# Who issues the stores of the weights' low parts: ScalarE, or the sync engine

## The chip, the cores and the metric

The kernel runs on one core of a Trainium2 chip. The metric is the time of one execution on the device in microseconds (us), median of several runs. The engines are TensorE (PE in the rows, PEld for its weight loads), VectorE (DVE), ScalarE (ACT), GpSimd (POOL) and the sync engine (SP), which here only issues DMAs. A "q" behind an engine's name (SPq, ACTq) marks what its sequencer does, such as issuing a DMA.

## What is computed

A cross-attention layer with a residual, then a mixture of experts with a residual. There are 2 x 1024 tokens of width 256, a context of 77 tokens per batch, 16 heads, 8 experts of which each token takes 2, and an inner width of 512:

```python
qp = jnp.einsum('bld,ed->ble', q, Wq)
scores = jnp.einsum('bld,bmd->blm', qp, kv)
idx = jnp.argmax(scores, axis=-1)
mem = jnp.take_along_axis(kv, idx[..., None], axis=1)
mkv = jnp.einsum('bld,ed->ble', mem, Wkv)
...
h = jnp.einsum('td,eid->tei', x, w1)
gate = jax.nn.silu(h[..., :INTER])
y = h[..., INTER:] * gate
out = jnp.einsum('tei,ehi,te->th', y, w2, combine)
...
x = x + _L0_xattn_ref(_layernorm(x, axis=-1), ctx_1024, L0_xattn_Wq, L0_xattn_Wkv, L0_xattn_Wc)
x = x + _L0_ffn_ref(_layernorm(x, axis=-1), L0_ffn_w1, L0_ffn_w2, L0_ffn_router_w)
```

`combine` holds the two largest router probabilities of each token. The expert products are made from split operands: a weight is a rounded high part in `W` (fp32r) and a remainder in bf16, the low part.

## The kernel before

**Two phases.** The first is attention and router, over `NH` = 4 groups of 512 tokens. The second takes 39 blocks of 128 gathered rows, each with one expert. It needs all weights in both parts.

**Slots.** In the first phase PE, DVE and ACT each run through a hand-written order: `for u in range(-1, NH + 1): for p in range(SLOTS)` with `SLOTS` = 10. In turn u the engines work on the logits and sums of group u, prepare group u + 1 and finish group u - 1 (`post`). Slot s here means (u + 1) * 10 + p. Each engine works in its own order and waits on semaphores; no engine looks ahead past a wait.

**The weights' split.** The expert weights come in as `NC` = 48 chunks of 128x512 fp32 (`raw`). In slot n, as the last thing of the slot, ACT's `high(n)` copies chunk n, rounded, to `W` (line 481) and raises `hi_ok`. GpSimd's split n (line 411) subtracts it from `raw` and writes the low part to buffer n % 2 of `low`, raising `low_ok`. `W` lies two chunks before `raw` in the same memory, so copy n overwrites what split n - 2 reads: copy n has to come behind split n - 2. Two slots later `high(n + 2)` issues the store of low part n to `lows` in DRAM (line 477, 128 KB) from ACT's queue. GpSimd's split n + 2 writes the same buffer and waits until that store has landed (`low_out`). GpSimd also makes a reciprocal root (line 428) once per group, between the splits of slots 23 and 24, 33 and 34, 43 and 44: it feeds the normalisation on DVE (line 719).

**The sync engine** first issues all input loads (the 48 raw chunks as 8 transfers), then two stores of padding (lines 341 and 342). Then for v = 0, 1, 2 it runs `keep_residual(v)` and `keep_rows(v)`: it waits for group v's residual sum (`x2_ok`, made in slot 10v + 24) and stores 512 KB from `X`, then waits for its router result (`rows_ok`, made by DVE's line 761 in slot 10v + 30) and stores 528 KB from `xr`. Behind them it waits for all low stores and loads the low parts of the first weights back to `W1lo` (line 362); it stores the last group's residual, loads the low parts of the second weights (line 369) and stores the last rows. The second phase starts when PE has all of this and GpSimd's first gathers (line 448) have landed.

Of the kernel before, what the change touches and what calls it, by code (L numbers as in the profile page):

```python
# [24 lines left out]
F32 = mybir.dt.float32  # L25
F32R = mybir.dt.float32r
F16 = mybir.dt.float16
BF16 = mybir.dt.bfloat16
I32 = mybir.dt.int32
U32 = mybir.dt.uint32  # L30
ALU = mybir.AluOpType
ACT = mybir.ActivationFunctionType
AX = mybir.AxisListType
ds = bass.ds

P = 128
# [7 lines left out]
NH = T // HT  # L44
# [11 lines left out]
BLK = 2 * S * B // P + E - 1  # L56
GR = 4
LAST = (BLK - 1) // GR
CW = 512
WC1 = DC * 2 * FI // CW  # L60
WC2 = FC * D // CW
EC = WC1 + WC2
NC = E * EC
SCALE = 0.25
MASK = -1e30
EPS = 1e-5
assert HT >= GR and DH ** -0.5 == SCALE


SLOTS = NP + 2  # L70
# [7 lines left out]
P2_AT = 4  # L78
# [14 lines left out]
def build(nc, x, ctxT, Wq, WqT, WkvT, WcT, routerT, w, out):  # L93
    rows = nc.dram_tensor("rows", [(T + 1) * P, RW], F32).ap()
    lows = nc.dram_tensor("lows", [NC, P, CW], BF16).ap()
    with ExitStack() as ctx:
        def sb(name, shape, dt=F32):
            return ctx.enter_context(nc.sbuf_tensor(name, shape, dt))

        def sem(name):  # L100
            return ctx.enter_context(nc.semaphore(name))
# [77 lines left out]
        idf = sb("idf", [P, BLK])  # L179
        idx = sb("idx", [P, BLK], U32)  # L180

        low = sb("low", [P, 2, CW], BF16)


        with nc.sbuf_tensor("raw", [P, NC + 2, CW], F32) as raw:
# [1 line left out]
        W = sb("W", [P, NC + 2, CW], F32R)  # L187
# [45 lines left out]
        raw_in = [sem(f"raw_in{e}") for e in range(E)]  # L233
        hi_ok = sem("hi_ok")
        low_ok = sem("low_ok")
        low_out = [sem(f"low_out{i}") for i in range(2)]
        low_in = sem("low_in")
        iotas = sem("iotas")
        consts = sem("consts")
# [86 lines left out]
        @block.sync  # L326
        def _(sp):
            sp.dma_start(X[:, 0:TB, :], x[0:S, :].rearrange("(t p) d -> p t d", p=P)).then_inc(x_in[0], 16)
            sp.dma_start(CT, ctxT.rearrange("(c p) n -> p c n", p=P)).then_inc(wts_in, 16)
            sp.dma_start(WQ[:], Wq.rearrange("(c p) n -> p c n", p=P)).then_inc(wts_in, 16)  # L330
            sp.dma_start(WKV[:], WkvT.rearrange("(c p) n -> p c n", p=P)).then_inc(wts_in, 16)
            sp.dma_start(WQT[:], WqT.rearrange("(c p) n -> p c n", p=P)).then_inc(wts_in, 16)
            sp.dma_start(WC[:], WcT.rearrange("(c p) n -> p c n", p=P)).then_inc(wts_in, 16)
            sp.dma_start(RT[:], routerT.rearrange("(c p) n -> p c n", p=P)).then_inc(wts_in, 16)
            sp.dma_start(X[:, TB:T, :], x[S:2 * S, :].rearrange("(t p) d -> p t d", p=P)).then_inc(x_in[1], 16)
            for e in range(E):
                sp.dma_start(raw[:, 2 + e * EC:2 + (e + 1) * EC, :], w[e * EC:(e + 1) * EC].rearrange("n p w -> p n w")
                             ).then_inc(raw_in[e], 16)

            sp.wait_ge(pad_ok, 1)  # L340
            sp.dma_start(rows[T * P:(T + 1) * P, :], xr[:, 0, :]).then_inc(rows_out, 16)
            sp.dma_start(out[T * P:(T + 1) * P, :], xr[:, 0, 0:D]).then_inc(rows_out, 16)

            def keep_residual(v):
                sp.wait_ge(x2_ok, v * 2 + 2)
                sp.dma_start(out[ds(v * (HT * P), HT * P), :].rearrange("(t p) d -> p t d", p=P),
                             X[:, ds(v * HT, HT), :]).then_inc(x2_out, 16)

            def keep_rows(v):
                sp.wait_ge(rows_ok, v + 1)  # L350
                sp.dma_start(rows[ds(v * (HT * P), HT * P), :].rearrange("(t p) d -> p t d", p=P),
                             xr[:]).then_inc(rows_out, 16)

            with sp.Fori(0, NH - 1) as v:
                keep_residual(v)
                keep_rows(v)

            for j in range(2):
                sp.wait_ge(low_out[j], 16 * NC // 2)
            sp.wait_ge(l2_mm, NH * NP)  # L360
            for e in range(E):
                sp.dma_start(W1lo[:, e * WC1:(e + 1) * WC1, :],
                             lows[e * EC:e * EC + WC1].rearrange("n p w -> p n w")).then_inc(low_in, 16)
            keep_residual(NH - 1)

            sp.wait_ge(x2_out, 16 * NH)
            sp.wait_ge(xn2_ok, T)
            for e in range(E):
                sp.dma_start(W2lo[:, e * WC2:(e + 1) * WC2, :],
                             lows[e * EC + WC1:(e + 1) * EC].rearrange("n p w -> p n w")).then_inc(low_in, 16)  # L370
            keep_rows(NH - 1)


        @block.gpsimd
        def _(pool):
            def iota(t, pattern, mult=0, start=0):
                pool.iota(t, pattern=pattern, base=start, channel_multiplier=mult,
                          allow_small_or_imprecise_dtypes=True).then_inc(iotas, 1)

            iota(iota_f[:], [[1, P]])  # L380
            iota(iota_p[:], [[0, 1]], 1)
            iota(iota_h[:], [[1, P]])
            iota(blk_h[:], [[1, BLK]])
            iota(blk_f[:], [[1, BLK]])
            iota(tok_h[:], [[P, T]], 1, 1)
            iota(k128[:], [[P, T]])
            iota(desc[:], [[-1, NK]], 0, NK)
            iota(desc_e[:], [[-1, E]], 0, E)
            iota(cum[:], [[1, E], [-1, E]])
            iota(spare[:], [[0, 1]], 1, T * P + 1)  # L390
            pool.memset(half[:], -0.5).then_inc(iotas, 1)

            pool.wait_ge(iotas, 12)
            for b in range(B):
                pool.wait_ge(ln_v, b + 1)
                pool.tensor_tensor(rs[:, b * TB:(b + 1) * TB], rs[:, b * TB:(b + 1) * TB], half[:, 0:TB], ALU.pow
                                   ).then_inc(ln_r, 1)

            def split(i, j, first):
                n = i * 2 + j
                pool.wait_ge(iotas, 12)
                pool.wait_ge(hi_ok, n + 1)
                if not first:
                    pool.wait_ge(low_out[j], i * 16)
                if first:
                    was, high = raw[:, n + 2, :], W[:, n, :]
                else:
                    was, high = (a.rearrange("p a w -> p (a w)") for a in (raw[:, ds(n + 2, 1), :], W[:, ds(n, 1), :]))  # L410
                pool.tensor_tensor(low[:, j, :], was, high.bitcast(F32), ALU.subtract).then_inc(low_ok, 1)  # L411

            def splits(start, stop):
                with pool.Fori(start // 2, stop // 2) as i:
                    for j in range(2):
                        split(i, j, False)

            for j in range(2):
                split(0, j, True)
            done = 2  # L420
            for v in range(NH):

                until = min(NC, (v + 2) * SLOTS + P2_AT)
                if until > done:
                    splits(done, until)
                    done = until
                pool.wait_ge(v2_ok, v + 1)
                pool.tensor_tensor(rs2[:], rs2[:], half[:, 0:HT], ALU.pow).then_inc(rs2_ok, 1)

            pool.wait_ge(idx_ok, 1)
            pool.wait_ge(rows_out, 16 * (2 * B + 2))
            pool.wait_ge(x2_out, 16 * 2 * B)

            def at_rows(b):
                return bass.IndirectOffsetOnAxis(ap=idx[:, b:b + 1], axis=0)

            for b in range(BLK + GR):
                if b >= GR:  # L440
                    c = b - GR
                    pool.wait_ge(ob_ok, c + 1)
                    if c >= 1:
                        pool.wait_ge(sc_out, 16 * c)
                    pool.indirect_dma_start(out=out, out_offset=at_rows(c), in_=ob[:, c % GR, :], in_offset=None,  # L445
                                            compute_op=ALU.add).then_inc(sc_out, 16)
                if b < BLK:
                    pool.indirect_dma_start(out=xg[:, b % GR, :], out_offset=None, in_=rows, in_offset=at_rows(b)  # L448
                                            ).then_inc(g_in[b % GR], 16)
            pool.wait_ge(sc_out, 16 * BLK)  # L450
# [3 lines left out]
        def _(act):  # L454
# [16 lines left out]

            def high(n):

                if 2 <= n < NC + 2:

                    act.wait_ge(low_ok, n - 1)
                    act.dma_start(lows[n - 2], low[:, n % 2, :]).then_inc(low_out[n % 2], 16)
                if n < NC:
                    if n % EC == 0:
                        act.wait_ge(raw_in[n // EC], 16)  # L480
                    act.copy(W[:, n, :], raw[:, n + 2, :]).then_inc(hi_ok, 1)  # L481
# [92 lines left out]
            step(0, True, False)  # L574
            with act.Fori(1, LAST) as i:
                step(i, False, False)
# [666 lines left out]
```

## Time and profile before

| what | value |
|---|---|
| median of 3 runs | 467.67 us (467.65 to 468.54) |
| span of the profiled execution | 468.0 us |
| PE busy | 376.7 us, 80% |
| DVE busy | 221.9 us, 47% |
| ACT busy | 197.3 us, 42% |
| GpSimd busy | 171.6 us, 37% |

The profile is one execution, recorded instruction by instruction. Its chain of waits is followed back from the last instruction: at each step to what released it. Times in the timelines are us from the start of the span. The first phase ends at about 234 us, the second begins at about 251 us. A row of a timeline gives start, duration, engine, line, operation, output and inputs, how many, and in brackets how long the engine sat idle before and what released it. PEclk is the granted clock of TensorE as a share of full speed; about 0.5 is 1.2 GHz and 1.0 is 2.4 GHz.

### The profile page before, as it was taken

How to read it: one execution, taken by the hardware profiler on the slowest of the kernel's cores; microseconds unless marked ns; L12 is line 12 of the kernel's file. 1: busy time of each engine (PE TensorE's matmuls, PEld its weight loads, DVE VectorE, ACT ScalarE, POOL GpSimd, SP SyncE). 2: the span in 40 equal slices, each digit the busy share in tenths (PEclk: the TensorE clock that was granted, in tenths of full speed). 3: DMA queues.
4: the chain of work that ended last, by engine and by line, in shares of the span. 5: the costliest groups of instructions: out<-in, count | busy, mean ns of one | idle time of the engine just before them, and what ended most of it. 6: DMA issues, size and time to landing. Idle time of an engine off the chain costs nothing.

```text
span 468.0 us, 7576 instructions
## 1 busy us (share of the span) xinstructions
PE 376.7 (80%) x2262; PEld 282.8 (60%) x2263; DVE 221.9 (47%) x535; ACT 197.3 (42%) x376; POOL 171.6 (37%) x148
## 2 busy tenths in 40 slices
PE   1758688879999988765514999999999999999980
PEld 1647565558677655343513677777777777677760
DVE  4576734545674764543382344344344344343430
ACT  0324546666657664420101444444444444344330
POOL 2021633433333353320003245545545545544521
PEclk9967979999979998876555999999999999999986
DMA  8999110111212112229611032332332332332320
GB/s 266 386 387 336 57 34 34 46 45 35 69 45 82 68 57 87 73 91 349 223 48 46 8 62 47 57 57 46 55 59 46 51 63 46 47 67 46 50 32 11
DMA packets 35317, 43.44 MB, mean 93 GB/s; under 512 B 3200, under 2 KB 27904, under 8 KB 35296
## 3 DMA queue, kind: packets, MB, share of 16 engines
q1 hardware_dynamic: 20896, 26.49, 16.5%
q0 software_dynamic: 7488, 10.39, 13.6%
q10 hardware_dynamic: 6912, 6.29, 4.0%
q8 instruction: 12, 0.20, 0.2%
q14 instruction: 9, 0.07, 0.0%
HBM read 27.23 MB, written 15.93 MB: 92 GB/s over the span
## 4 chain that ended last, share of the span: by engine, by line
PE 74%; DVE 12%; ACT 4%; issue 4%; DMA 2%; POOL 1%; SPq 1%; DVEq 0%; POOLq 0%; ACTq 0%
PE ps L1155 24%; PE ps L1166 12%; PE ps L1173 4%; PE ps L985 4%; PE ps L972 4%; PE ps L1064 3%; PE ps L998 3%; PE ps L1017 3%; PE ps L1019 3%; PE ps L1032 3%; PE ps L1045 2%; PE ps L1141 2%; PE ps L1078 2%; ACT qs L509 1%; PE ps L943 1%
## 5 line engine op out<-in xcount | busy, mean ns | idle before, releaser
L445 POOL DMA_INDIRECT out_x<-oT,idx x39 | 61.8, 1586 | 98.8 <-ACT oT L558 98.8
L411 POOL TENSOR_TENSOR low<-raw,W 128x512 bf16 (+1 forms) x48 | 62.0, 1295 | 95.4 <-DMA lows<-low 79.6
L1155 PE MATMUL ps<-W,qs 128*128 x312 | 83.6, 411 | 1.2 <-DVE qs L884 1.2
L1155 PEld LDWEIGHTS ps<-W,qs 128*128 128x128 f32 x312 | 57.4, 191 | 13.2 <-issue 1.6
L890 DVE TENSOR_TENSOR uT<-uT,ps 128x512 f32<-128x512 f32 x39 | 26.8, 687 | 69.9 <-ACT uT L564 69.9
L564 ACT ACTIVATE uT<-ps 128x512 f32<-128x512 f32 x39 | 23.4, 599 | 85.9 <-PE ps L1155 85.9
L448 POOL DMA_INDIRECT xr<-rows,idx x39 | 38.7, 991 | 38.5 <-DVE idx L874 26.9
L894 DVE TENSOR_TENSOR qs<-ps,mT 128x512 fp32r<-128x512 f32 x39 | 27.0, 692 | 49.3 <-ACT mT L570 49.3
L1155 PE MATMUL ps<-W1lo,xpT 128*128 x156 | 41.3, 388 | 0.0
L693 DVE TENSOR_REDUCE mx<-ps 128x8 f32<-128x616 f32 x32 | 25.5, 798 | 32.7 <-PE ps L998 32.6
L488 ACT ACTIVATE pT<-ps 77x1024 f32<-77x1024 f32 x32 | 32.7, 1022 | 13.7 <-PE ps L1019 13.7
L985 PE MATMUL ps<-ident,qs 128*128 128x128 f32 x128 | 21.9, 297 | 13.5 <-DVE qs L684 8.8
L1166 PE MATMUL ps<-W,mT 128*128 x156 | 28.7, 307 | 2.0 <-DVE xpT L895 2.0
L481 ACT CAST W<-raw 128x512 fp32r<-128x512 f32 x48 | 29.8, 621 | 0.2
L1017 PE MATMUL ps<-qT,bd 128*77 128x512 f32 x64 | 29.3, 458 | 0.5 <-ACT pT L488 0.3
L558 ACT ACTIVATE oT<-ps,xr 128x256 f32<-128x256 f32 x39 | 18.5, 474 | 24.2 <-PE ps L1166 23.3
L1173 PE MATMUL ps<-ident,uT 128*128 128x128 f32 x156 | 24.3, 278 | 5.0 <-issue 3.9
L985 PEld LDWEIGHTS ps<-ident,qs 128*128 128x128 f32 x128 | 15.5, 151 | 19.6 <-DVE qs L684 16.8
L1019 PE MATMUL ps<-mT,neg 128*77 128x512 f32 x64 | 26.1, 408 | 0.0
L1166 PE MATMUL ps<-W,qs 128*128 x156 | 25.3, 285 | 0.0
L998 PEld LDWEIGHTS ps<-bd,qT 128*128 128x128 f32 x128 | 19.9, 203 | 8.6 <-issue 4.2
L494 ACT CAST qT<-ps 128x512 fp32r<-128x512 f32 x32 | 18.8, 587 | 14.4 <-PE ps L985 14.3
(171 smaller groups left out, 641.9 us busy)
## 6 DMA issues: line engine op xcount, KB each, us to landing
raw<-in_w SPq DMA_DIRECT2D x8, 1536.0 KB, 17.0
lows<-low ACTq DMA_DIRECT2D x48, 128.0 KB, 1.7
W1lo<-lows SPq DMA_DIRECT2D x8, 512.0 KB, 7.7
rows<-xr SPq DMA_DIRECT2D x4, 528.0 KB, 3.3
X<-in_x SPq DMA_DIRECT2D x2, 1024.0 KB, 6.9
out_x<-X SPq DMA_DIRECT2D x4, 512.0 KB, 3.3
X<-lows SPq DMA_DIRECT2D x8, 256.0 KB, 4.4
xr<-rows,idx POOLq DMA_INDIRECT x39, 2.8
```

The lines of the kernel that those rows point to most:

```text
L411: pool.tensor_tensor(low[:, j, :], was, high.bitcast(F32), ALU.subtract).then_inc(low_ok, 1)
L445: pool.indirect_dma_start(out=out, out_offset=at_rows(c), in_=ob[:, c % GR, :], in_offset=None, compute_op=ALU.add).then_inc(sc_out, 16)
L448: pool.indirect_dma_start(out=xg[:, b % GR, :], out_offset=None, in_=rows, in_offset=at_rows(b)).then_inc(g_in[b % GR], 16)
L481: act.copy(W[:, n, :], raw[:, n + 2, :]).then_inc(hi_ok, 1)
L488: act.activation(pT[0:NK, 2 * (n % 4):2 * (n % 4) + 2, :], ps[0:NK, 0:2, :], ACT.Exp).then_inc(ex_ok, 1)
L985: mm = pe.transpose(ps[:, 5, n * P:(n + 1) * P], qs[:, a:a + 2, :].rearrange("p h w -> p (h w)"), ident[:])
L998: mm = pe.matmul(ps[:, 6 + n // 2, (n % 2) * 2 * NK:(n % 2 + 1) * 2 * NK], qT[:, w % 2, 4 * g + n, t * P:(t + 1) * P], bd[:, w // 2, :], s ...
L1017: pe.matmul(ps[0:NK, o, :], bd[:, u // 2, o * NK:(o + 1) * NK], qT[:, u % 2, p, :], start=True, stop=False)
L1019: mm = pe.matmul(ps[0:NK, o, :], neg[:, 2 * p + o:2 * p + o + 1].broadcast_to([P, NK]), mT[:], start=False, stop=True)
L1155: mm = pe.matmul(ps[:, f, :], part[:, c * P:(c + 1) * P], chunk(wts, e * per + (2 * c + f)), start=(k == 0 and c == 0), stop=(k == 2 and c ...
L1166: mm = pe.matmul(ps[:, 4, 0:D], part[:, c * P:(c + 1) * P], w2, start=(k == 0 and c == 0), stop=(k == 2 and c == FC - 1))
L1173: mm = pe.transpose(ps[:, 3, c * P:(c + 1) * P], yb[:, c * P:(c + 1) * P], ident[:])
```

## The change

ACT's `high(n)` no longer issues stores. It keeps the wait on `low_ok` in front of copy n, because of the overlap of `W` and `raw`. The sync engine issues the 48 stores instead, each behind a wait on `low_ok`, written out between its other transfers: 22 stores before the first residual, then 4, the first rows, 6, the second residual, 4, the second rows, 6, the third residual, 4, the third rows, and the last 2. The number of buffers has a name now, `LR`, and stays 2. GpSimd's splits are written out one by one instead of in a loop; each waits for `hi_ok` and for the store of the part two before.

```diff
+            def keep_lows(start, stop):
+                for n in range(start, stop):
+                    sp.wait_ge(low_ok, n + 1)
+                    sp.dma_start(lows[n], low[:, n % LR, :]).then_inc(low_out[n % LR], 16)
+
+            kept = 0
+            for v in range(NH - 1):
+                keep_lows(kept, min(NC, (v + 2) * SLOTS + 2))
                 keep_residual(v)
+                keep_lows(min(NC, (v + 2) * SLOTS + 2), min(NC, (v + 2) * SLOTS + P2_AT + 2))
+                kept = min(NC, (v + 2) * SLOTS + P2_AT + 2)
                 keep_rows(v)
-
-            for j in range(2):
-                sp.wait_ge(low_out[j], 16 * NC // 2)
+            keep_lows(kept, NC)
+
+            for j in range(LR):
+                sp.wait_ge(low_out[j], 16 * NC // LR)
...
             def splits(start, stop):
-                with pool.Fori(start // 2, stop // 2) as i:
-                    for j in range(2):
-                        split(i, j, False)
-
-            for j in range(2):
-                split(0, j, True)
-            done = 2
+                for n in range(start, stop):
+                    pool.wait_ge(hi_ok, n + 1)
+                    if n >= LR:
+                        pool.wait_ge(low_out[n % LR], 16 * (n // LR))
+                    pool.tensor_tensor(low[:, n % LR, :], raw[:, n + 2, :], W[:, n, :].bitcast(F32), ALU.subtract
+                                       ).then_inc(low_ok, 1)
+
+            done = 0
...
             def high(n):

-                if 2 <= n < NC + 2:
-
-                    act.wait_ge(low_ok, n - 1)
-                    act.dma_start(lows[n - 2], low[:, n % 2, :]).then_inc(low_out[n % 2], 16)
                 if n < NC:
+                    if n >= 2:
+                        act.wait_ge(low_ok, n - 1)
                     if n % EC == 0:
                         act.wait_ge(raw_in[n // EC], 16)
                     act.copy(W[:, n, :], raw[:, n + 2, :]).then_inc(hi_ok, 1)
```

The sync engine's instructions from the padding to the loads of `W1lo`, before (lines 346 to 351 are a loop of three turns):

```order
L341 DMA rows<-xr 128x264 [waits pad_ok]
L342 DMA out_x<-xr 128x256
L354 UNCONDITIONAL_BRANCH
L354 ISA
L346 ISA [waits x2_ok]
L346 REGISTER_ALU
L346 DMA out_x<-X 128x4x256
L350 REGISTER_ALU
L351 ISA [waits rows_ok]
L351 DMA rows<-xr 128x4x264
```

The same stretch of the changed kernel, up to the second rows (its lines are two or more further down):

```order
L343 DMA rows<-xr 128x264 [waits pad_ok]
L344 DMA out_x<-xr 128x256
L359 DMA lows<-low 128x512 [waits low_ok] x22
L348 DMA out_x<-X 128x4x256 [waits x2_ok]
L359 DMA lows<-low 128x512 [waits low_ok] x4
L353 DMA rows<-xr 128x4x264 [waits rows_ok]
L359 DMA lows<-low 128x512 [waits low_ok] x6
L348 DMA out_x<-X 128x4x256 [waits x2_ok]
L359 DMA lows<-low 128x512 [waits low_ok] x4
L353 DMA rows<-xr 128x4x264 [waits rows_ok]
```

Low parts 26 and 27 now stand behind the first rows (`rows_ok`), 36 and 37 behind the second, 22 and 23 behind the first residual, and the first low part stands behind the two stores of padding.

ACT at the end of slot 30 and in slot 31, before (`qT` and `qs` belong to the preparation of group 3, `pT` to the exponentials of group 2):

```order
L477 DMA lows<-low 128x512 [waits low_ok]
L481 CAST W<-raw 128x512 [waits raw_in5]
L494 CAST qT<-ps 128x4x128 [waits q_tr]
L488 ACTIVATE pT<-ps 77x1024 [waits pv_mm,l2_mm]
L509 CAST qs<-ps 128x16x2x16 [waits q_tr,q_mm]
L516 COPY oT<-ps 128x512 [waits o_tr]
L477 DMA lows<-low 128x512 [waits low_ok]
L481 CAST W<-raw 128x512
```

And in the changed kernel:

```order
L480 CAST W<-raw 128x512 [waits raw_in5,low_ok]
L493 CAST qT<-ps 128x4x128 [waits q_tr]
L487 ACTIVATE pT<-ps 77x1024 [waits pv_mm,l2_mm]
L508 CAST qs<-ps 128x16x2x16 [waits q_tr,q_mm]
L515 COPY oT<-ps 128x512 [waits o_tr]
L480 CAST W<-raw 128x512 [waits low_ok]
```

The issues are gone, and the wait on `low_ok`, which stood on the issue, now stands on the copy; what follows the copy is unchanged.

## Rows read from the trace of the kernel before

**Rows 1.** The page: the chain of waits by engine, and GpSimd's splits.

```profile
PE 74%; DVE 12%; ACT 4%; issue 4%; DMA 2%; POOL 1%; SPq 1%; DVEq 0%; POOLq 0%; ACTq 0%
...
L411 POOL TENSOR_TENSOR low<-raw,W 128x512 bf16 (+1 forms) x48 | 62.0, 1295 | 95.4 <-DMA lows<-low 79.6
```

**Rows 2.** The page's DMA issues: count, KB each, median us to landing.

```profile
lows<-low ACTq DMA_DIRECT2D x48, 128.0 KB, 1.7
...
rows<-xr SPq DMA_DIRECT2D x4, 528.0 KB, 3.3
...
out_x<-xr SPq DMA_DIRECT2D x1, 128.0 KB, 11.9
```

**Rows 3.** Timeline, slots 30 and 31, group 0's router result.

```profile
139.02 0.62 ACT L481 CAST W<-raw 128x512 fp32r<-128x512 f32 x1
...
139.54 0.58 ACT L494 CAST qT<-ps 128x512 fp32r<-128x512 f32 x1
...
139.72 0.19 DVE L761 TENSOR_TENSOR xr<-ex,sme 128x32 f32<-128x32 f32 x1
...
140.08 0.39 SPq L351 DMA_DIRECT2D rows<-xr  x1
...
140.55 1.02 ACT L488 ACTIVATE pT<-ps 77x1024 f32<-77x1024 f32 x1 [0.43 <-PE ps L1019]
...
141.86 0.58 ACT L509 CAST qs<-ps 128x512 fp32r<-128x512 f32 x1 [0.29 <-PE ps L972]
...
142.96 0.66 PE L985 MATMUL ps<-ident,qs 128*128 128x128 f32 x4 [0.70 <-DVE qs L684]
```

**Rows 4.** Timeline, the start: the stores of padding, splits 2 and 3.

```profile
34.76 2.75 SPq L342 DMA_DIRECT2D out_x<-xr  x1
...
47.27 2.55 POOL L411 TENSOR_TENSOR low<-raw,W 128x512 bf16 x2 [4.14 <-DMA lows<-low]
```

**Rows 5.** Windows: busy per engine, PEclk, DMA share, GB/s, behind 194 us.

```profile
194.00:198.00 4.00, 3.39 (x16) 1.86 (x16) 1.15 (x4) 1.63 (x3) 0.00 (x0) 0.57 0.12 37
```

**Rows 6.** Timeline, slots 40 and 41, group 1's router result.

```profile
170.62 1.31 DVE L740 TENSOR_TENSOR eq<-rl,r 128x32 f32<-128x32 f32 x1
...
172.28 0.62 ACT L481 CAST W<-raw 128x512 fp32r<-128x512 f32 x1
...
174.57 1.02 ACT L488 ACTIVATE pT<-ps 77x1024 f32<-77x1024 f32 x1 [1.67 <-PE ps L1019]
...
177.75 0.19 DVE L761 TENSOR_TENSOR xr<-ex,sme 128x32 f32<-128x32 f32 x1
...
177.91 0.78 PE L1017 MATMUL ps<-qT,bd 128*77 128x512 f32 x1
```

**Rows 7.** Timeline: splits 39 and 40 beside the router, and the router step alone.

```profile
133.16 0.18 DVE L740 TENSOR_TENSOR eq<-rl,r 128x32 f32<-128x32 f32 x1
...
172.78 2.51 POOL L411 TENSOR_TENSOR low<-raw,W 128x512 bf16 x2 [0.90 <-DMA lows<-low]
```

**Rows 8.** Timeline: residual stores, splits and normalisation of groups 0 and 2.

```profile
117.74 0.42 SPq L346 DMA_DIRECT2D out_x<-X  x1
...
121.54 1.37 DVE L719 TENSOR_SCALAR xr<-X,mv,rs 128x256 f32<-128x256 f32 x4
...
189.24 0.38 SPq L346 DMA_DIRECT2D out_x<-X  x1
...
191.23 2.53 POOL L411 TENSOR_TENSOR low<-raw,W 128x512 bf16 x2
...
191.29 3.26 DVE L719 TENSOR_SCALAR xr<-X,mv,rs 128x256 f32<-128x256 f32 x4 [0.38 <-POOL rs L428]
```

**Rows 9.** Timeline, the end of the first phase and the first gather.

```profile
207.96 7.83 SPq L362 DMA_DIRECT2D W1lo<-lows  x8
...
224.51 3.97 SPq L369 DMA_DIRECT2D X<-lows  x8
...
248.23 1.19 POOL L448 DMA_INDIRECT xr<-rows,idx  x1 [26.92 <-DVE idx L874]
```

More of the change, by code:

```diff
@@ L58 @@
 LAST = (BLK - 1) // GR
+LR = 2
 CW = 512
@@ L66 @@
 EPS = 1e-5
+assert NC % LR == 0
 assert HT >= GR and DH ** -0.5 == SCALE
@@ L180, in build @@
         idx = sb("idx", [P, BLK], U32)
-        low = sb("low", [P, 2, CW], BF16)
+        low = sb("low", [P, LR, CW], BF16)
         with nc.sbuf_tensor("raw", [P, NC + 2, CW], F32) as raw:
@@ L235, in build @@
         low_ok = sem("low_ok")
-        low_out = [sem(f"low_out{i}") for i in range(2)]
+        low_out = [sem(f"low_out{i}") for i in range(LR)]
         low_in = sem("low_in")
@@ L352, in keep_rows @@
                              xr[:]).then_inc(rows_out, 16)
-            with sp.Fori(0, NH - 1) as v:
+            def keep_lows(start, stop):
[5 more added lines that the diff above has]
+                keep_lows(kept, min(NC, (v + 2) * SLOTS + 2))
                 keep_residual(v)
+                keep_lows(min(NC, (v + 2) * SLOTS + 2), min(NC, (v + 2) * SLOTS + P2_AT + 2))
+                kept = min(NC, (v + 2) * SLOTS + P2_AT + 2)
                 keep_rows(v)
-            for j in range(2):
-                sp.wait_ge(low_out[j], 16 * NC // 2)
+            keep_lows(kept, NC)
+            for j in range(LR):
+                sp.wait_ge(low_out[j], 16 * NC // LR)
             sp.wait_ge(l2_mm, NH * NP)
@@ L397, in _ @@
                                    ).then_inc(ln_r, 1)
[L401 to L411, printed above, removed]
-            def splits(start, stop):
-                with pool.Fori(start // 2, stop // 2) as i:
-                    for j in range(2):
-                        split(i, j, False)
-            for j in range(2):
-                split(0, j, True)
-            done = 2
+            def splits(start, stop):
+                for n in range(start, stop):
[5 more added lines that the diff above has]
+            done = 0
             for v in range(NH):
```

## The prediction, made before the changed kernel ran

> **What bounds the kernel now.** I read the chain of waits by engine first: TensorE holds 74% of it, VectorE 12%, ScalarE 4%, and all DMAs 2% [rows 1]. So the stores of the low parts aren't what ends the time, although the splits sat idle for 79.6 us behind them: GpSimd is not on the path, and most of that idle time is free. The second thing to see is the order of one slot. ScalarE's copy of chunk n is followed by work that TensorE waits for within a microsecond or two [rows 3]. If the copy is late, TensorE is late. Before the change a store waited only for its own low part and for ScalarE's turn, never for the sync engine's other work.
>
> **What the change takes away.** 48 issues on ScalarE. In the trace an issue lies beside the activation ahead of it, and the copy starts about half a microsecond behind that activation's start with or without it. I put 0.0 to 0.1 us on each, and nearly all of ScalarE's slots have idle time in front of their next step, so of a possible 4.8 us I count 0.3 us as gained. GpSimd's splits start about a microsecond earlier, since a store leaves when the part is ready; that by itself shortens nothing, as they are off the chain.
>
> **What it moves: low parts 26, 27, 36 and 37 behind the rows.** This is the large term. The sync engine issues in order. It reaches the store of part 26 only after it has issued the first rows, and those wait for DVE's line 761 in slot 30. Split 28 writes the buffer of part 26, so it waits for that store. Copy 30 overwrites what split 28 reads, so it waits for split 28. ScalarE's copy 30 stands ahead of its `qT`, exponential and `qs` steps of slot 31. Step by step for group 0 [rows 3]:
> Line 761 ends at 139.91 us. The splits 28 and 29, which ran beside that router chain before, now wait; where a split ran beside it, steps of it were 1 us long instead of 0.2 [rows 7]. Here a late matmul ahead of it bounds it, so I move it by only 0.15 us, and the rows are issued at 139.9. They land 3.3 us later [rows 2]. Part 26 follows on the same queue, 0.4 us of further transfer (its 128 KB at the pace of the 512 KB): 143.6. The split takes 1.27 us, with 0.15 us for each of two semaphores: copy 30 starts at 145.2 instead of 139.02, and `qT` at 145.7. Now the exponential, which waited for TensorE before, follows at once: 146.2, and `qs` at 147.2 instead of 141.86. TensorE's next transposes (142.96) need it, so they come **5.3 us later**. The other side: if the store of part 26 doesn't queue behind the rows, it lands 0.4 + 1.7 us after them, at 142.0, and the delay is 3.7 us. I take 5.3, because a transfer of 128 KB that stood behind others on this queue, the padding's, took 11.9 us to land where one on ScalarE's queue took 1.7 [rows 2].
> The Trainium skill ("DMA: Bandwidth & Descriptors", section "Queues, rings and completion order") says that a DMA engine takes descriptors in ring order within a queue and goes round-robin between the queues of different issuers; the same section warns that completion is not first-in-first-out. By the first the delay is 5.3 us, by the second alone it could be the 3.7 us; the 11.9 us row agrees with the first.
>
> **TensorE's clock after the stop.** TensorE stands for some 6 us there. Behind a shorter stop (TensorE waited there for the normalisation that ended at 194.55) the granted clock was 0.57 for 4 us [rows 5, 8], about the lower level of 1.2 GHz. 4 us at 0.57 instead of 1.0 cost 4 x 0.43 = **1.7 us**. The bounds are 0 (it was already low shortly before, in slots 28 and 29) and twice that.
>
> **Group 1, slot 40.** The same four steps with other numbers [rows 6]. Copy 40 was made at 172.28, but line 761 only at 177.75, 5.5 us later: the chain of the router ran beside splits 37 to 40, and three of its steps take 1.1 to 1.3 us there, as the one of 1.31 us [rows 6], which takes 0.18 alone [rows 7]. In the changed kernel splits 38 to 40 can't run there, so this chain is about 3.0 us shorter: rows issued at 175.0 (in times of the old trace), part 36 landed at 178.7, split 38 done at 180.1, copy 40 at 180.2. The exponential, before at 174.57, comes at 180.7 and ends at 181.7; TensorE's next logits need it and start at 181.75 instead of 177.91: **3.8 us later**. So here the gain on DVE is already netted. Without that gain it would be 6.8, without queueing behind the rows 2.2. The low clock comes once in either case.
> On this collision the Trainium skill ("SBUF — State Buffer", section "Who interferes with whom") says that DVE's `tensor_tensor` with two SBUF inputs and GpSimd's reads lock each other out for a whole instruction; the rows agree, 1.2 us being about one split.
>
> **Low parts behind the residuals.** Parts 22, 32 and 42 wait for the residual's issue and then for its 512 KB: 3.3 + 0.4 = 3.7 us. For group 2 this is a gain. The residual goes at 189.24, so split 44 starts at about 193.0. Before, splits 44 and 45 ran at 191.23, beside the normalisation at 191.29, which took 3.26 us instead of the 1.37 of group 0 [rows 8]. It becomes free: 1.9 us, and TensorE's stop behind it shrinks by as much, so that the low clock behind it should not come: its 3.39 busy us at 0.57 [rows 5] would be 1.5 us shorter. Copy 46 then waits half a microsecond for split 44. Together **-2.9 us** (0 to -3.4). For groups 0 and 1 it is the other way round: the residual at 117.74 plus 3.7 is 121.4, and the normalisation stands at 121.54. Splits 24 and 25 now fall on it. It would take up to 3.26 instead of 1.37 us, of which TensorE's order hides about 0.9: **+1.0 us each, +2.0** (0 to 2.5).
>
> **The start.** Part 0 is now issued behind the padding. That was issued at 34.76 and landed 11.9 us later, at 46.7 [rows 2, 4]. Part 0 lands at about 47.1, and split 2, which before started at 47.27, starts at about the same time [rows 4]. I count 0; if the queue is 2 us longer than that, copy 4 stops and it costs up to 2 us. The splits of slots 4 to 7 move against a DVE chain there: -0.5 to +0.5, counted as 0.
>
> **The end.** Parts 46 and 47 go behind the last rows, so the loads of `W1lo` start 4 us later than 207.96. The first gather is at 248.23 [rows 9], and the last of all loads is issued by 228.5; this cover of some 20 us, less a landing of about 5, hides them, and I count 0. Were it gone, the 4 us would be paid in full.
>
> **The sum**: 5.3 + 1.7 + 3.8 - 2.9 + 2.0 - 0.3 = 9.6 us on the profiled span of 468.0 us, so 477.6. The median is 0.33 lower than that span, and I take 0.3 off for it: 477.3 us.
>
> **Rivals.**
> *The store doesn't queue behind the rows.* The pause is real, but the two stops are 3.7 and 2.2 instead of 5.3 and 3.8: 474.1. Splits 24 and 34 then run earlier and miss the normalisation: 472. Against it stands the padding's 11.9 us.
> *The start backs up as well.* The padding's issue alone took 2.75 us [rows 4], so the queue is full there. Two to three us more: 480.
> *The change does what it says*, each store goes when its part is there, and nothing waits for rows. It can't for parts 26, 27, 36 and 37: the order of the sync engine's instructions is fixed. It could only be harmless if ScalarE had enough idle time, but 0.43 and 0.29 us stand in slot 31 [rows 3]. That gives no change, 467.7.
> *Faster: DVE freed of the splits decides.* One mechanism: the splits are held back just where they lay beside the router and the normalisation. At slot 40 this gives 3.0 us and at 191 us 2.9, so 462 us if the stops cost nothing. It decides if the split that ends a stop comes less than about 1 us after the router's result, against the 5.1 us worked out.
>
> **How the numbers follow.** The forecast of 477.3 has 0.70, the rival without queueing 0.14 (472 to 474), the backed-up start 0.07, no effect 0.03, faster 0.06. The range takes in the forecast with its bounds (the clock term 0 to 3.4, the collisions 0 to 2.5) and the upper part of the rival without queueing: 472 to 481. A measurement of this kernel can tell about 0.2%, or 0.9 us, from no change. Slower by more than that: 0.91; same 0.04; faster 0.05.
>
> **What would show it.** In the changed kernel's timeline: copies 30 and 40 each directly behind a split, that split directly behind a low store, that one behind the rows, with TensorE idle for about 6 us at slot 31 and 7 us at slot 41. The router steps of 1.2 us at slot 40 should be gone and the normalisation of group 2 back at 1.4 us, those of groups 0 and 1 longer. The landing of parts 26 and 36 should be some 3.3 us after their issue, others 1.7. I'd be wrong if those copies are not late, if part 26 lands in 1.7 us, or if TensorE finds other work.

## The result, and the profile after

The changed kernel took 478.0 us in the median of 4 runs (474.94 to 481.15), beside 468.11 us (467.65 to 472.69) of the kernel before: a ratio of 1.0152, 95% interval 1.0099 to 1.0204. Ratios and their intervals here are taken from executions in the chip's faster state alone and are not the quotient of the two medians, which would be 1.021. The profiled execution has a span of 477.6 us, 9.6 us more than the 468.0 of before.

The page of the changed kernel: the chain of waits by engine, GpSimd's splits and ScalarE's copies (now lines 418 and 480), and two kinds of DMA issues.

```profile
PE 73%; DVE 12%; ACT 4%; DMA 3%; issue 3%; POOL 1%; SPq 1%; DVEq 0%; ACTq 0%; POOLq 0%
...
L418 POOL TENSOR_TENSOR low<-raw,W 128x512 bf16<-128x512 f32 x48 | 61.4, 1285 | 104.5 <-ACT W L480 71.8
...
L480 ACT CAST W<-raw 128x512 fp32r<-128x512 f32 x48 | 29.8, 620 | 13.3 <-POOL low L418 13.1
...
lows<-low SPq DMA_DIRECT2D x48, 128.0 KB, 1.7
...
rows<-xr SPq DMA_DIRECT2D x4, 528.0 KB, 3.0
```

Against [rows 1] most splits no longer wait for a store but for ScalarE's copy (71.8 us): the stores do leave when their part is there. GpSimd is off the path in both kernels. The third row is the price: ScalarE sat idle 13.1 us in front of its copies because of a split, 2 times. Before, its copies had no such wait.

The first of the two, slot 30, in the timeline of the changed kernel (it answers to [rows 3]):

```profile
142.50 0.19 DVE L760 TENSOR_TENSOR xr<-ex,sme 128x32 f32<-128x32 f32 x1
...
142.72 0.37 SPq L353 DMA_DIRECT2D rows<-xr  x1
...
146.20 2.48 POOL L418 TENSOR_TENSOR low<-raw,W 128x512 bf16<-128x512 f32 x2 [12.98 <-DMA lows<-low]
...
147.49 0.62 ACT L480 CAST W<-raw 128x512 fp32r<-128x512 f32 x1 [5.58 <-POOL low L418]
...
149.41 0.58 ACT L508 CAST qs<-ps 128x512 fp32r<-128x512 f32 x1
...
150.50 1.11 PE L984 MATMUL ps<-ident,qs 128*128 128x128 f32 x4 [5.39 <-DVE qs L683]
```

Read the brackets from the top: split 28 waited 12.98 us for a store, copy 30 waited 5.58 us for the split, TensorE waited 5.39 us for the step behind the copy, where it had waited 0.70. Part 26 was issued at 143.13 and landed 2.9 us later. The second, slot 40 (it answers to [rows 6]):

```profile
185.37 0.19 DVE L760 TENSOR_TENSOR xr<-ex,sme 128x32 f32<-128x32 f32 x1
...
189.07 2.48 POOL L418 TENSOR_TENSOR low<-raw,W 128x512 bf16<-128x512 f32 x2 [9.44 <-DMA lows<-low]
...
190.37 0.62 ACT L480 CAST W<-raw 128x512 fp32r<-128x512 f32 x1 [7.56 <-POOL low L418]
...
191.96 0.71 PE L1016 MATMUL ps<-qT,bd 128*77 128x512 f32 x1 [6.54 <-ACT pT L487]
```

TensorE's clock behind the two stops, in the windows of the changed kernel (busy us and count of PE, PEld, DVE, ACT, POOL, then PEclk, DMA share, GB/s; compare [rows 5]):

```profile
145.50:150.50 5.00, 0.00 (x0) 0.00 (x1) 0.48 (x2) 3.01 (x6) 3.66 (x3) 0.87 0.25 82
150.50:154.50 4.00, 4.00 (x15) 3.36 (x16) 0.64 (x2) 2.10 (x3) 1.37 (x2) 0.50 0.21 68
154.50:158.50 4.00, 4.00 (x26) 2.77 (x24) 1.23 (x2) 2.99 (x5) 1.28 (x1) 0.81 0.01 2
...
191.90:195.90 4.00, 3.69 (x10) 2.29 (x11) 0.00 (x0) 2.91 (x6) 2.51 (x2) 0.50 0.27 93
```

TensorE did nothing for 5 us; then it worked for 4 us without a gap at 0.50, its lower level of 1.2 GHz, and had 0.81 over the next 4 us. In the kernel before, the clock was 1.00 over the same steps (142.96 to 154 us). Together that is 4 x 0.50 + 4 x 0.19 = 2.8 us of work, about the 2.6 us of the table below.

The shift of ScalarE's copies (copy n is the one of slot n) against the trace of before shows where the 9.6 us of this execution came from:

| stretch | shift at its end | what it added |
|---|---|---|
| start to slot 29 | +2.8 | 0.45 for group 0's normalisation, -0.4 at slot 18, and 2.8 that did not come again in the second trace (see `after_again`) |
| first stop, to the `qs` step of slot 31 | +7.5 | +4.7 |
| to copy 33 | +10.1 | +2.6, low clock |
| to copy 39 | +10.3 | +0.2, of it 0.45 for group 1's normalisation |
| second stop, to the logits of slot 41 | +14.0 | +3.7, with a router chain 2.7 us shorter |
| to copy 43 | +14.8 | +0.8, low clock |
| to the first gather | +11.7 | -3.1, group 2's normalisation |
| to the end | +9.6 | -2.1, not explained |

### The profile page after: what moved, and what is told of

It reads as the page before. It is cut to its first block, busy times and chain, and to the rows that moved or that the text cites. A ratio compares the mean times of both kernels' runs of the same rounds, so it can differ in the third digit from the quotient of the medians.

```text
span 477.6 us, 7363 instructions
## 1 busy us (share of the span) xinstructions
PE 379.3 (79%) x2262; PEld 286.0 (60%) x2263; DVE 218.5 (46%) x535; ACT 196.8 (41%) x376; POOL 171.3 (36%) x148
## 4 chain that ended last, share of the span: by engine, by line
PE 73%; DVE 12%; ACT 4%; DMA 3%; issue 3%; POOL 1%; SPq 1%; DVEq 0%; ACTq 0%; POOLq 0%
PE ps L1154 23%; PE ps L1165 11%; PE ps L1172 4%; PE ps L984 4%; PE ps L1063 4%; PE ps L971 4%; PE ps L1031 3%; PE ps L1016 3%; PE ps L997 3%; PE ps L1018 3%; PE ps L1044 2%; PE ps L1140 2%; PE ps L1077 2%; DVE xr L718 2%; PE ps L942 2%
## 5 line engine op out<-in xcount | busy, mean ns | idle before, releaser
L418 POOL TENSOR_TENSOR low<-raw,W 128x512 bf16<-128x512 f32 x48 | 61.4, 1285 | 104.5 <-ACT W L480 71.8
L1154 PE MATMUL ps<-W,qs 128*128 x312 | 83.2, 410 | 1.2 <-DVE qs L883 1.2
L984 PE MATMUL ps<-ident,qs 128*128 128x128 f32 x128 | 24.1, 320 | 17.9 <-DVE qs L683 13.5
L480 ACT CAST W<-raw 128x512 fp32r<-128x512 f32 x48 | 29.8, 620 | 13.3 <-POOL low L418 13.1
L984 PEld LDWEIGHTS ps<-ident,qs 128*128 128x128 f32 x128 | 17.1, 163 | 24.2 <-DVE qs L683 21.5
L997 PE MATMUL ps<-bd,qT 128*128 128x154 f32 x128 | 21.2, 292 | 5.2 <-DVE mx L692 4.1
```

The source lines that it names most:

```text
L418: pool.tensor_tensor(low[:, n % LR, :], raw[:, n + 2, :], W[:, n, :].bitcast(F32), ALU.subtract).then_inc(low_ok, 1)
L984: mm = pe.transpose(ps[:, 5, n * P:(n + 1) * P], qs[:, a:a + 2, :].rearrange("p h w -> p (h w)"), ident[:])
L997: mm = pe.matmul(ps[:, 6 + n // 2, (n % 2) * 2 * NK:(n % 2 + 1) * 2 * NK], qT[:, w % 2, 4 * g + n, t * P:(t + 1) * P], bd[:, w // 2, :], s ...
L1154: mm = pe.matmul(ps[:, f, :], part[:, c * P:(c + 1) * P], chunk(wts, e * per + (2 * c + f)), start=(k == 0 and c == 0), stop=(k == 2 and c ...
```

## The experiments

**The changed kernel again**, beside the three that follow. No edit.

> The changed kernel once more, on the chip of the three below. Order theory (a low part that stands behind the rows stops ScalarE's copies 30 and 40): copies 30 and 40 again directly behind a split, TensorE idle some 5.4 us at slot 31 and 6.5 us at slot 41; 475 to 480 us. The +2.8 us that the changed kernel already had before slot 30 and the -2.1 us of its second phase would be scatter of TensorE's clock: they should come out with other sizes here. If they belong to the change they come again.

Measured: 480.28 us (476.58 to 482.17) beside 470.52 of before, ratio 1.0183 (1.0085 to 1.0282). Line 760 of slot 30 ended 0.1 us later than in the trace of before, not 2.8. So most of those 2.8 us are scatter of one execution: 0.7 us were there at copy 0 already, and of the rest 1.2 us came between copies 9 and 11, with a clock of 0.51 from 57 to 71 us where the kernel before had 0.76. The two traces of before differ in the same way: from copy 0 to the first gather they took 214.6 and 217.4 us. From copy 29 on all came again: copies 30, 31, 33 and 40 at +5.8, +4.9, +7.5 and +15.5. The -2.1 us of the second phase came again too (217.5 us beside 219.8). The span of this execution is 474.8 us, 6.8 us above that of before and 1.4 us above that of the second trace of before (473.4): the total of a single execution is a poor measure here, and the stretches between copies are a good one.

**The low parts ahead of the rows.** The sync engine's order:

```diff
-                keep_lows(min(NC, (v + 2) * SLOTS + 2), min(NC, (v + 2) * SLOTS + P2_AT + 2))
-                kept = min(NC, (v + 2) * SLOTS + P2_AT + 2)
+                keep_lows(min(NC, (v + 2) * SLOTS + 2), min(NC, (v + 3) * SLOTS))
+                kept = min(NC, (v + 3) * SLOTS)
                 keep_rows(v)
```

> As the changed kernel, but the sync engine stores the low parts up to 29 (39) before it waits for the first (second) rows; the residuals keep their place. Order theory: copies 30 and 40 come right behind the step ahead of them, no stop of TensorE over 2.7 us; group 2's normalisation still free (1.4 us), groups 0 and 1's 2.8 and 1.8 us; 466 us (before 467.9, minus 2.9 for group 2, plus 0.9 for the two others). Issuer theory (the loss comes from the sync engine's queue, or from splits that now start earlier, whatever the order): 476 us or more. No-gain case of the forecast's DVE term: 469.

Measured: 464.91 us (463.09 to 465.98), ratio to before 0.9832 (0.9737 to 0.9926). Expected was 2 us less than before; in the medians of this job it is 5.6 us less, more than my terms give. Its timeline at slot 30:

```profile
141.71 0.62 ACT L480 CAST W<-raw 128x512 fp32r<-128x512 f32 x1
...
142.41 1.29 POOL L418 TENSOR_TENSOR low<-raw,W 128x512 bf16<-128x512 f32 x1 [2.65 <-ACT W L480]
...
142.44 1.30 DVE L760 TENSOR_TENSOR xr<-ex,sme 128x32 f32<-128x32 f32 x1
...
143.77 0.37 SPq L353 DMA_DIRECT2D rows<-xr  x1
```

The copy waits for nobody. The same sync engine issues the same 48 stores through the same queue; putting the low parts ahead of the rows is worth 13 us of the first phase in the traces (223.6 and 210.6 us from copy 0 to the first gather) and 15 in the medians. The issuer theory falls. One sees the collision as well: the last step of the router chain lies beside a split and takes 1.30 us instead of 0.19.

**Wait for the rows, but store the low parts first.**

```diff
+                sp.wait_ge(rows_ok, v + 1)
+                keep_lows(min(NC, (v + 2) * SLOTS + P2_AT + 2), kept)
                 keep_rows(v)
```

(with `kept` two higher).

> As the changed kernel, but behind the wait for the rows' result the two waiting low parts go first and the 528 KB of the rows after them. So the wait stays and only the queueing behind the transfer goes. If both make the stop (3.2 us from the rows' issue to the landing of part 26, of which a low store alone takes 1.7): part 26 lands 1.7 us after its issue, each stop is 1.5 us shorter, 474.5 us. If the wait alone makes it: as the changed kernel, 477.5. If the queueing alone makes it: 467 to 469.

Measured: 474.71 us (472.5 to 481.68), ratio 1.0067 (1.0013 to 1.0122), and the changed kernel in the same job 1.0183.

```profile
141.61 0.79 SPq L359 DMA_DIRECT2D lows<-low  x2
142.45 0.45 SPq L353 DMA_DIRECT2D rows<-xr  x1
143.47 2.48 POOL L420 TENSOR_TENSOR low<-raw,W 128x512 bf16<-128x512 f32 x2 [9.71 <-DMA lows<-low]
...
144.76 0.62 ACT L482 CAST W<-raw 128x512 fp32r<-128x512 f32 x1 [4.16 <-POOL low L420]
...
147.77 1.11 PE L986 MATMUL ps<-ident,qs 128*128 128x128 f32 x4 [4.17 <-DVE qs L685]
```

From the sync engine's first issue to the split it is 1.86 us here, and 3.48 us in the changed kernel. Of the difference of 1.6 us, 0.4 us is that the rows' issue no longer comes first, and 1.2 us that part 26 lands 1.7 us after its issue instead of 2.9: the queueing behind the rows' 528 KB. TensorE's stop is 4.17 instead of 5.39 us. So the stop has both causes, and the wait is the larger one.

**No store of a low part waits for anything but its own split:** the low parts also go ahead of the residual.

```diff
-                keep_lows(kept, min(NC, (v + 2) * SLOTS + 2))
+                keep_lows(kept, min(NC, (v + 2) * SLOTS + P2_AT))
                 keep_residual(v)
```

(with the rows as in `rows_last`).

> As rows_last, and the low parts up to 23 (33, 43) go before the residual too, so that no low part waits for anything but itself. Order theory with the collisions: splits 24, 25, 34, 35 run before the normalisation of groups 0 and 1 (1.4 us again), but 44 and 45 fall on group 2's again (3.3 us instead of 1.4, and the low clock behind it); about 468 us, the same as the kernel before. If the collisions cost nothing it is equal to rows_last within 0.5 us. Issuer theory: 476 us or more.

Measured: 465.78 us (462.88 to 466.42), ratio 0.9843 (0.9746 to 0.9939), 2 us less than I expected and the same as `rows_last` within their scatter. Groups 0 and 1's normalisation took 2.35 us, not the 1.4 expected: splits 24 and 34 come ahead of it now, but 25 and 35 follow at once. The collision that I expected at group 2 is there:

```profile
189.76 2.53 POOL L418 TENSOR_TENSOR low<-raw,W 128x512 bf16<-128x512 f32 x2
189.83 3.26 DVE L718 TENSOR_SCALAR xr<-X,mv,rs 128x256 f32<-128x256 f32 x4 [0.39 <-POOL rs L429]
...
193.15 0.66 PE L1044 MATMUL ps<-ident,xr 128*128 128x128 f32 x4 [2.76 <-DVE xr L718]
```

and its first phase is 2.6 us longer than that of `rows_last` (213.2 and 210.6 us from copy 0 to the first gather). Between single executions that scatter by 2.8 us this alone would prove little. But from copy 45 to the first gather, where group 2's normalisation lies, `both_last` takes as long as before (+0.02 us) and `rows_last` 3.1 us less, and the next one shows the same.

**GpSimd held for the normalisation**, on `both_last`:

```diff
                 pool.tensor_tensor(rs2[:], rs2[:], half[:, 0:HT], ALU.pow).then_inc(rs2_ok, 1)
+                if done < NC:
+                    pool.wait_ge(xn2_ok, (v + 1) * HT)
```

> As both_last, and GpSimd waits for the group's normalisation (xn2_ok) before it goes on with splits 24, 34 and 44. Collision theory: the normalisation takes 1.4 us in all groups, so group 2's 3.3 us of both_last and the low clock behind it go (3 us), and groups 0 and 1's 2.35 us too (0.3 us each): 462 us where both_last has 465.8. The other side: the held splits come 2 us later and stop copy 26, 36 or 46; then 466 or more.

> The kernel free once more beside before, in five rounds: 463 to 465 us and a ratio of 0.98 to 0.99 to before. If its distance was that chip's scatter, the ratio is within 0.995 to 1.005.

Measured: 463.88 us (462.86 to 465.05), ratio 0.983 (0.977 to 0.9891), and again 462.75 us (460.49 to 464.94), ratio 0.9845 (0.9794 to 0.9895), six runs on another chip. From the second trace:

```profile
191.08 1.38 DVE L720 TENSOR_SCALAR xr<-X,mv,rs 128x256 f32<-128x256 f32 x4 [0.39 <-POOL rs L429]
192.51 0.66 PE L1046 MATMUL ps<-ident,xr 128*128 128x128 f32 x4 [0.87 <-DVE xr L720]
192.53 2.53 POOL L418 TENSOR_TENSOR low<-raw,W 128x512 bf16<-128x512 f32 x2 [1.49 <-DVE xr L720]
```

TensorE's wait goes from 2.76 to 0.87 us, and from copy 45 to the first gather this trace takes 3.2 us less than before, where `both_last` took as long. This version has the lowest medians; it beats the kernel before by 1.6% and the changed one by about 3%. That it beats `rows_last` or `both_last` in the time is not shown: the intervals overlap.

**GpSimd's splits written out alone**, the stores still issued by ScalarE: the kernel before with the changed kernel's `splits`.

> The kernel before with GpSimd's splits written out one by one, as in the changed kernel, and nothing else: ScalarE issues the stores. Order theory: this part of the change does nothing, 468 to 470 us on a chip on which before has 468 to 470, within 0.3% of it; the splits still start behind the stores. If the written-out splits are what makes rows_last and both_last 1.6% faster than before, this has it too, 463 us.

Measured: 470.08 us, ratio 0.9999 (0.9956 to 1.0042). Within 0.4% this part of the change does nothing to the time. So the 1.6% of `both_last` are not due to the written-out splits; by exclusion they come with the move of the issues to the sync engine. What in that move brings them is open (see the last section).

**The kernel before again.**

> The kernel before once more, for a second trace of it. In the changed kernel and its three variants the stretch from the first gather to the end took 217.1 to 217.8 us, in the one trace of before 219.8. If that is scatter of the clock, a second trace of before shows some 217.5 us; if it belongs to ScalarE's issues it shows 219.8 again. Time by the timing: equal to before, within 0.5%.

Measured: 473.93 us (469.96 to 477.25), ratio 1.0022 (0.9975 to 1.0069). The second phase took 219.5 us, near the 219.8 of the first trace. That does not make it a matter of ScalarE's issues, as my expectation had it: in `only_first` and `only_second` below, where the sync engine issues all stores, it took 219.2 and 219.5 us. More under "what the runs showed".

**A third buffer.**

```diff
-LR = 2
+LR = 3
```

(three small arrays of the routing are laid into `pT` to make room; nothing is computed otherwise).

> The changed kernel with LR = 3, in its own order of the sync engine's stores (three small routing arrays are laid into pT to make room). Order theory: split 28 has a buffer of its own, split 29 waits for the store of part 26, so copy 31 waits where copy 30 did; it was due 2.7 us behind the rows' issue and is ready 5 us behind it. Each stop shrinks from 4.7 and 6.5 us to 2 to 3 us, some 4.5 us less in all: 473 us. If the stop is not due to the buffer behind the rows: as the changed kernel, 477.5 or more.

Measured: 478.21 us (477.03 to 478.86), ratio 1.0145 (1.0086 to 1.0203) on a chip on which before had 471.48. The time missed my 473.

```profile
143.78 0.37 SPq L351 DMA_DIRECT2D rows<-xr  x1
...
147.24 3.86 POOL L416 TENSOR_TENSOR low<-raw,W 128x512 bf16<-128x512 f32 x3 [10.79 <-DMA lows<-low]
148.66 0.62 ACT L478 CAST W<-raw 128x512 fp32r<-128x512 f32 x1 [1.46 <-POOL low L416]
...
190.11 3.78 PE L1061 MATMUL ps<-WC,oT 128*128 128x256 f32 x8
...
200.80 3.26 DVE L716 TENSOR_SCALAR xr<-X,mv,rs 128x256 f32<-128x256 f32 x4 [0.37 <-POOL rs L427]
```

The stop moved by one slot, as expected: copy 31 waits now, 1.46 us instead of the 5.58 of copy 30. Over both stops (copies 29 to 33 and 39 to 43) the trace lost 2.3 us against before, where the changed kernel lost 11.7. But the spare buffer also takes the protection from group 2: split 44 no longer waits behind the residual and falls on the normalisation (3.26 us), and of the 3.1 us that the changed kernel had gained there only 1.5 are left; and in this execution TensorE was at its lower clock at 190 us (3.78 us for eight matmuls, else about 1.9), and copy 44 lost 3.4 us. I had counted the first effect only. From copy 29 to the first gather this trace is 4.7 us shorter than that of the changed kernel, near the 4.5 expected, but as 9.4 us gained at the stops and some 5 lost behind them. Why the median is no shorter is open: the other three executions have no trace.

**Each stop by itself.** In `only_first` parts 26 and 27 stand behind their rows and all others ahead; in `only_second` parts 36 and 37.

```diff
+                held = P2_AT + 2 if v == 0 else SLOTS
+                keep_lows(min(NC, (v + 2) * SLOTS + 2), min(NC, (v + 2) * SLOTS + held))
+                kept = min(NC, (v + 2) * SLOTS + held)
```

> As rows_last, but low parts 26 and 27 stand behind the first rows again, as in the changed kernel; 36, 37 and the rest go ahead of theirs. It prices the first stop by itself. By the forecast's terms (5.3 us and 1.7 us of low clock) it is 7.0 us above rows_last, some 472 us where rows_last has 465; by the changed kernel's trace (a stop of 4.7 us and 2.6 us until copy 33) 7.3 us. If the two stops share one cause that shows only with both, it is within 2 us of rows_last.

> As rows_last, but low parts 36 and 37 stand behind the second rows, and 26 and 27 go ahead of the first. It prices the second stop. In the changed kernel copy 41's step came 3.4 us later than the shift of copy 39, with the router chain 3 us shorter; rows_last has two slow router steps (2.0 us) of the three of before, so over rows_last this should be 3.4 + 3.0 - 1.0 = 5.4 us net, some 470 us. Both prices together (7.0 + 5.4 = 12.4) should be the distance of the changed kernel from rows_last, 13.0 us in the traces' first phase. Less than 2 us would mean that the stop costs nothing once the router runs free.

Measured: 472.35 us (ratio 1.004, 0.9994 to 1.0086) and 472.13 us (1.0039, 0.9997 to 1.008), before 470.85 on this chip. The ratio of `rows_last` was 0.9832: by the ratios each stop costs 2.1%, by the medians 7.4 and 7.2 us, by the traces' first phase (219.9 and 218.1 beside 210.6 us) 9.3 and 7.5. `rows_last` ran in another job, and a whole first phase holds scatter from before the stops, so these prices are good to a few us only. The shift between the copies around a stop is sharper. In us against the trace of before, and each kernel's other stretches beside it:

| stretch | changed | changed, again | `only_first` | `only_second` | `rows_last` | `swap` |
|---|---|---|---|---|---|---|
| copies 29 to 33, first stop | +7.25 | +7.27 | +7.25 | +0.16 | -0.11 | +5.00 |
| copies 39 to 43, second stop | +4.48 | +4.48 | -1.12 | +4.48 | -1.21 | +2.21 |
| copies 43 to 45 | -0.01 | +0.03 | -0.01 | +2.02 | -0.01 | 0.00 |
| copy 45 to the first gather | -3.13 | -3.16 | -3.16 | -3.16 | -3.13 | -3.04 |

So the first stop costs 7.25 + 0.11 = 7.4 us over `rows_last` (expected 7.0 to 7.3), the second 4.48 + 1.21 = 5.7 (expected 5.4). The 2.02 us of `only_second` are no part of its stop in the changed kernel. From the trace of `only_second`:

```profile
178.88 2.48 POOL L419 TENSOR_TENSOR low<-raw,W 128x512 bf16<-128x512 f32 x2 [9.45 <-DMA lows<-low]
180.17 4.70 SPq L359 DMA_DIRECT2D lows<-low  x4
180.17 0.62 ACT L481 CAST W<-raw 128x512 fp32r<-128x512 f32 x1 [7.56 <-POOL low L419]
181.76 0.20 PEld L1017 LDWEIGHTS ps<-qT,bd 128*77 128x77 f32 x1 [6.78 <-ACT pT L488]
```

The wait of 7.56 us is that of the changed kernel to the hundredth. Each stop comes with its own order and without the other, and by the table the two add up: each costs alone what it costs beside the other.

## Why the prediction was right, point by point

The median was forecast at 477.3 us (472 to 481) and came out at 478.0. As a change the forecast was 9.6 us or 2.1%; measured were ratios of 1.0152 (1.0099 to 1.0204) and, in the next job, 1.0183 (1.0085 to 1.0282). So the direction, the size and the mechanism are right, and the agreement to 0.7 us is partly luck.

- **The order of the sync engine decides.** Shown: `rows_last` takes the stops away by order alone, `only_first` and `only_second` bring back one each.
- **First stop, 5.3 us forecast, 4.7 measured.** The rows and part 26 land a little sooner than by the rows I used (3.0 instead of 3.3 us for 528 KB, and 2.9 from part 26's issue where I had named some 3.3 as the sign): from the rows' issue to split 28 it took 3.48 us where I had 3.85, to copy 30 4.77 where I had 5.3. TensorE sat idle for 5.4 and 6.5 us in the two stops, where I had written about 6 and 7.
- **Does the low part queue behind the rows?** Yes: part 26 took 2.9 us to land behind the rows and 1.7 in `swap`. The rival without queueing falls. It had put the queueing at 1.6 us for a stop (5.3 against 3.7); it is 1.2 us, for 0.4 of the 1.6 us that `swap` takes away are the rows' issue.
- **Low clock behind it, 1.7 forecast, 2.6 measured.** I had taken 0.57 for 4 us from a shorter wait; it was 0.50 for 4 us and 0.81 for 4 more. Another 0.8 us came behind the second stop, for which my sum had no term: the kernel before had 0.66 over the 4 us there and the changed one 0.50. With 3.4 us measured for 1.7 in all, the clock is the term I mis-sized most; it lies at the upper bound that I gave.
- **Second stop, 3.8 us forecast, 3.7 measured**, and its part on DVE: the router chain shorter by 3.0 forecast, 2.7 measured; each of the steps that a split had stretched takes 0.19 us again, for the held splits no longer lie beside it [rows 7].
- **Group 2's normalisation, -2.9 forecast, -3.1 measured.** It ran in 1.38 us, and the clock behind it was 1.00 (207.9 to 211.9 us), where the kernel before had 0.57. The half microsecond for which I let copy 46 wait did not come. `both_last` and `free` show the collision with and without the splits.
- **Groups 0 and 1, +1.0 us each forecast, 0.45 each measured.** Splits 24 and 25 did fall on them, but the normalisation took 2.76 us, not 3.26: the split had started 0.6 us ahead of it, and only the rest stood in the way. Of the 1.38 us that this added, TensorE's order hid 0.9, as I had it.
- **The issues on ScalarE, 0.3 us counted as gained.** No stretch shows them. But every kernel whose sync engine issues the stores gains 0.4 us at slot 18, where a step of DVE (line 678, in the changed kernel 677) takes 1.00 instead of 1.44 us because the split beside it comes earlier. That earlier splits shorten nothing was wrong by this much.
- **The start and the end.** The start and end cost nothing, as counted: split 2 began 1.57 us behind copy 2 (before 3.3 behind it), and the late loads of `W1lo` (at 222.59) held nobody. The second phase's 2.1 us were in no term.

Two things that I had not counted cancelled in the profiled execution: 2.8 us of scatter ahead of slot 30, less the 0.4 us of slot 18, and the 2.1 us of the second phase. The measured terms (4.7 + 2.6 + 0.9 + 3.7 + 0.8 - 3.1 = 9.6, with 0.45 twice for the normalisations) come to the 9.6 us that I forecast because the errors in them cancel: the stops, the collisions and the gain of ScalarE's issues were too large, the clock too small by 1.7 us. And 9.6 us is the loss of the first phase; with the shorter second phase, which both traces of the changed kernel have, it is some 7 us, near what the two ratios give (7 and 9 us).

## What to carry to other kernels

If several transfers share an issuing engine, go through what stands behind each of its waits. A small store that frees a buffer must not stand behind a wait for a result of a later stage: whoever needs the buffer then waits for that result too. Moving the issue to an idle engine is only half of the edit; its place between that engine's waits is the other half, and here, in one job, it decided between +1.8% and -1.7%. Then look where GpSimd's elementwise work falls in time: each small DVE step that falls on a split took about as long as the split, so holding GpSimd back for one DVE step can shorten the stretch (by 3.2 us at group 2).

## What the runs showed of the hardware that I had not expected

**Small DVE steps beside a split.** A router step of 0.19 us takes 0.9 to 1.3 us when a split of 1.27 us runs beside it. In the kernel before it happened at three steps of group 1's chain (1.31, 1.10 and 1.20 us) [rows 6, 7] and at one of group 0's, in both of its traces, and never in the two traces of the changed one.

**Scatter of the clock.** The same kernel keeps the lower clock for longer or shorter stretches from one execution to the next: over the same slots the kernel before had 0.76 in one trace (57 to 71 us) and 0.51 in the other (60 to 74 us), and copies 9 to 17 took 1.5 us longer there. Two executions of the kernel before differ by 2.8 us in the first phase (214.6 and 217.4 us from copy 0 to the first gather), and the runs of before in the last job spread from 467.07 to 477.74 us. A difference below 1% needs many runs of this kernel.

**The second phase is 2 us shorter in some traces, without a change in its instructions.** From the first gather to the end the thirteen traces fall into groups, and the granted clock goes with them:

| traces | clock, 3 to 13 us behind the first gather | clock, last 20 us | second phase, us |
|---|---|---|---|
| the kernel before (two), `unroll` | 0.60 to 0.61 | 0.65 to 0.73 | 218.5 to 219.8 |
| `only_first`, `only_second` | 0.60 | 0.65 to 0.66 | 219.2, 219.5 |
| `lr3` | 0.61 | 0.83 | 218.9 |
| the changed kernel (two), `rows_last`, `swap`, `both_last`, `free` (two) | 0.71 to 0.76 | 0.80 to 0.82 | 217.0 to 217.8 |

The first 10 us of it in the kernel before, in its second trace, in the changed kernel and in `only_second`:

```profile
251.23:261.23 10.00, 7.75 (x23) 4.75 (x24) 1.45 (x3) 3.77 (x7) 1.67 (x2) 0.61 0.14 41
```

```profile
256.87:266.87 10.00, 7.46 (x22) 4.70 (x24) 1.45 (x3) 3.74 (x7) 1.67 (x2) 0.60 0.15 41
```

```profile
262.91:272.91 10.00, 7.47 (x26) 5.08 (x27) 2.02 (x4) 3.91 (x7) 1.67 (x2) 0.71 0.15 41
```

```profile
254.72:264.72 10.00, 7.48 (x22) 4.72 (x24) 1.45 (x3) 3.76 (x7) 1.67 (x2) 0.60 0.15 41
```

10 us at 0.71 instead of 0.61 hold 1.0 us more work, about half of the 2.1; the end of the phase has a share that I can't price, since TensorE works for only 6 to 7 of the last 20 us. Why the clock recovers sooner there isn't shown. It does not follow from who issues the stores: the sync engine does in `only_first`, `only_second` and `lr3` as well. So it is open how much of the 1.6% of `both_last`, `rows_last` and `free` over the kernel before comes from the issues leaving ScalarE, from splits that start earlier, or from this. By the terms of the traces I can account for the normalisation (3.1 us), the router steps and the 0.4 us of slot 18 only; and `both_last` and the second trace of `free` also lack a stretch of low clock ahead of slot 30 that the kernel before has (1.00 against 0.50 from 132.8 to 139.6 us), but so does `unroll`, which is no faster.
